# Merged counts and comparisons on VectorE, and a GpSimd wait for landed transfers, in a two-layer graph network kernel

## What is computed

```python
# layer 0: a max over the edges of each src
msg = relu(x@W_m1.T[src] + x@W_m2.T[dst] + edge_attr@W_me.T + biases)
msg = relu(msg @ W_net.T + b_net)
agg = segment_max(msg, src)            # 0 where a node has no edge
x   = layernorm(x + x@W_o1.T + b_o1 + agg@W_o2.T + b_o2)
# layer 1: a sum over the edges of each dst
h   = gelu(concat(x[src], x[dst]) @ eW1 + eb1) @ eW2 + eb2
agg = segment_sum(h, dst)
x   = layernorm(x + gelu(concat(x, agg) @ nW1 + nb1) @ nW2 + nb2)
```

## Time and profile before

| | |
|---|---|
| median of 3 runs | 3422.4 us (3416.85 to 3427.18) |
| the profiled execution | 3427.05 us, its span 3425.3 us |
| TensorE busy | 2516.2 us, 73%; mean granted clock 0.81 of full |
| GpSimd busy | 1717.8 us, 50% |
| VectorE busy | 1784.0 us, 52% |
| ScalarE busy | 1400.1 us, 41% |
| DMA | 294.49 MB, mean 86 GB/s |

### The profile page before, as it was taken

The page is one execution under the profiler, slowest core; times in us unless marked ns, Lnnn a source line. Parts: engine busy times, 40 slices in busy tenths (PEclk is TensorE's granted clock), DMA queues, the critical chain, the costliest instruction groups (busy, mean ns, idle before and its releaser), DMA issues. The chain is left out here.

```text
span 3425.3 us, 78136 instructions
## 1 busy us (share of the span) xinstructions
PE 2516.2 (73%) x20612; PEld 2180.0 (64%) x20613; DVE 1784.0 (52%) x7747; ACT 1400.1 (41%) x3974; POOL 1717.8 (50%) x1843
## 2 busy tenths in 40 slices
PE   6777765666677777778759974777777777777787
PEld 5666654555566666666547764766666677666777
DVE  7655544443355555555547752444445445454456
ACT  2344333333355555555547751232333233233334
POOL 5455544555545545554231225656655655555544
PEclk8777666766688888888879996787888878888788
DMA  7323323211133343434759931111111111111111
GB/s 205 85 73 74 75 64 83 65 34 43 51 105 111 111 111 112 119 113 138 205 163 277 280 98 42 44 40 41 42 42 40 43 40 41 39 39 40 41 32 39
DMA packets 368367, 294.49 MB, mean 86 GB/s; under 512 B 241708, under 2 KB 335986, under 8 KB 368002
## 3 DMA queue, kind: packets, MB, share of 16 engines
q1 hardware_dynamic: 138944, 129.88, 13.6%
q0 software_dynamic: 54176, 96.13, 10.0%
q10 hardware_dynamic: 175010, 65.62, 7.6%
HBM read 170.05 MB, written 127.82 MB: 87 GB/s over the span
## 5 line engine op out<-in xcount | busy, mean ns | idle before, releaser
L1386 POOL DMA_INDIRECT edge_in_src_order<-ring_u,ring_p x784 | 769.9, 982 | 728.2 <-issue 509.4
L2090 POOL DMA_INDIRECT a_rows<-src_table,src_c x782 | 739.5, 946 | 540.4 <-SPq L2106 316.5
L2213 ACT ACTIVATE h<-ps_h 128x512 f32<-128x512 f32 x208 | 124.2, 597 | 822.6 <-remote 597.5
L2134 DVE TENSOR_SCALAR ohd_f<-niota,dloc_c 128x128 f32<-128x128 bf16 x832 | 185.2, 299 | 391.0 <-remote 177.7
L2181 PE MATMUL ps_s<-ohd_f,h 128*128 128x128 f32 x1664 | 286.7, 318 | 124.1 <-issue 85.7
L2172 PE MATMUL ps_h<-bpart,dstT_b 128*128 x1664 | 300.6, 338 | 104.7 <-ACT dstT_b L2207 81.4
L1478 DVE TENSOR_TENSOR_SCAN top<-same,top,bank 96x512 f32<-96x512 bf16 x221 | 281.7, 1274 | 180.7 <-remote 104.9
L1634 PEld LDWEIGHTS bank<-m,dstT 128*128 128x128 f32 x1568 | 270.5, 248 | 161.4 <-issue 160.2
L1421 DVE TENSOR_TENSOR prior<-bank,earlier 128x512 f16<-128x512 f32 x196 | 134.9, 688 | 438.1 <-remote 384.7
L1634 PE MATMUL bank<-m,dstT 128*128 x1568 | 291.7, 335 | 87.2 <-issue 65.3
L2167 PE MATMUL ps_h<-a_rows,ident 128*128 x1664 | 282.9, 317 | 92.9 <-issue 91.7
(11 more groups left out here) (352 smaller groups left out, 5048.6 us busy)
## 6 DMA issues: line engine op xcount, KB each, us to landing
u_in<-edge_in_src_order SPq DMA_DIRECT2D x222, 192.0 KB
running_max<-row ACTq DMA_DIRECT2D x222, 192.0 KB
rowt<-src_row SPq DMA_DIRECT2D x222, 128.0 KB
running_max<-zero_rows ACTq DMA_DIRECT2D x37, 576.0 KB
same<-same_src_row SPq DMA_DIRECT2D x222, 96.0 KB
edge_in_src_order<-ring_u,ring_p POOLq DMA_INDIRECT x784
a_rows<-src_table,src_c POOLq DMA_INDIRECT x782
dge_attributes_by_column<-in_edge_attrT SPq DMA_DIRECT2D x8, 784.0 KB, 12.0
```

What stands on the lines that cost most here:

```text
L1386: pool.indirect_dma_start(u_d, bass.IndirectOffsetOnAxis(ring_p[:, j:j + 1], 0), ring_u[:, j, :], None).then_inc(sent[i % 4], 16)
L2090: pool.indirect_dma_start(a_rows[:, c % (4 * RING), :], None, a_d, bass.IndirectOffsetOnAxis(src_c[:, c:c + 1], 0)).then_inc(got[g % RING] ...
L2134: last = v.tensor_scalar(ohd[:, u, j, :], niota[:], dloc[:, u, j:j + 1], None, ALU.is_equal)
```

## The change

Four edits:

1. In the placing stage the four `tensor_tensor_reduce` of a group become one `tensor_tensor` multiply over all 4x64 counts (`picked_counts`, placed before `coarse`) and one `tensor_reduce` over the last axis (`across_steps`). `junk2` becomes fp32. `place_chain` goes up by 2 a group, not 4, and TensorE's `count` waits only until the multiply of the group in front has read `ps_cnt`.
2. GpSimd, in the placing stage, waits ahead of the third DMA of a group until all four DMAs of the group in front have landed.
3. The same in layer 1's gather.
4. In layer 1 the four comparisons of a group become one `tensor_tensor` (128x512) with both inputs broadcast.

```diff
-                junk2 = sb(until_d, "junk2", [P, 4, SL], BF16)
+                junk2 = sb(until_d, "junk2", [P, 4, SL])
@@ GpSimd, placing
                             for j in range(4 * (i % RG), 4 * (i % RG) + 4):
+                                if j % 4 == 2 and i:
+                                    pool.wait_ge(sent[(i - 1) % 4], 64 * ((i - 1) // 4 + 1))
+                                    pass_waits(pool, passed)
@@ VectorE, placing
+                        def picked_counts(i, u, n):
+                            dve.wait_ge(cnt_ready, i + 1)
+                            wait(dve, place_chain, 2 * i)
+                            v.tensor_tensor(junk2[:].rearrange("p (c j) a -> p c j a", j=2), ps_cnt[:, 0:4, :].rearrange("p (c j) a -> p c j a", j=2),
+                                            ohlo[:, u].rearrange("p c a j -> p c j a"), ALU.mult).then_inc(place_chain, 1)
+
                         def across_steps(i, u, n):
-                            dve.wait_ge(cnt_ready, i + 1)
-                            for j in range(4):
-
-                                v.tensor_tensor_reduce(junk2[:, j, :], ps_cnt[:, j, :], ohlo[:, u, j // 2, :, j % 2], 1.0, 0.0,
-                                                       ALU.mult, ALU.add, across[:, u, j:j + 1]).then_inc(place_chain, 1)
+                            dve.wait_ge(place_chain, 2 * i + 1)
+                            v.tensor_reduce(across[:, u], junk2[:], AX.X, ALU.add).then_inc(place_chain, 1)
@@ put
-                            dve.wait_ge(place_chain, 4 * (i + 1))
+                            dve.wait_ge(place_chain, 2 * (i + 1))
@@ order
-                        order = [("d", 4, scan), ("c", 3, advance), ("c", 3, same_step), ("c", 3, coarse), ("c", 4, across_steps), ("c", 3, fine),
+                        order = [("d", 4, scan), ("c", 3, advance), ("c", 3, same_step), ("c", 4, picked_counts), ("c", 3, coarse), ("c", 4, across_steps), ("c", 3, fine),
@@ TensorE, count
-                            wait(pe, place_chain, 4 * i)
+                            wait(pe, place_chain, 2 * i - 1)
@@ GpSimd, layer 1
                             for c in range(4 * g, min(4 * g + 4, NC)):
+                                if c % 4 == 2 and g:
+                                    pool.wait_ge(got[(g - 1) % RING], 64 * ((g - 1) // RING + 1))
+                                    pass_waits(pool, passed)
@@ VectorE, layer 1, onehot
-                            for j in range(4):
-                                last = v.tensor_scalar(ohd[:, u, j, :], niota[:], dloc[:, u, j:j + 1], None, ALU.is_equal)
-                            last.then_inc(oh_ready, 1)
+                            v.tensor_tensor(ohd[:, u], bcast(niota[:].unsqueeze(1), P, 4, P), bcast(dloc[:, u, :].unsqueeze(2), P, 4, P),
+                                            ALU.is_equal).then_inc(oh_ready, 1)
```

More of the change, by code:

```diff
@@ L1659, in net @@
                             if isinstance(i, int) and i == KS + 1:
-                                pe.wait_ge(place_chain, 4 * CG)
+                                pe.wait_ge(place_chain, 2 * CG)
                             pe.wait_ge(msg_ready, i + 1)
```

## The result

| | before | after |
|---|---|---|
| median of 13 runs each | 3422.4 us | 3404.6 us |
| ratio, 95% interval | | 0.9944 [0.9929, 0.996] |
| the profiled execution, its span | 3425.3 us | 3395.3 us |
| placing, first to last indirect DMA | 1484.1 us | 1465.3 us |
| layer 1, first to last indirect DMA | 1265.8 us | 1257.7 us |

The change made the kernel 18 us faster, 0.56%. The forecast was 3427 us, 5 us slower. The time lies inside the wide range (3275 to 3470 us), but outside the forecast's own (3412 to 3445 us), and the change went the other way. Of the 30 us between the two profiled executions, 19 lie in the placing stage and 8 in layer 1. The 98 gathers between these stages take the same time in both (303 and 304 us).

A forecast was written before the change was run, and what follows sets the result against it. It took long runs of GpSimd's indirect DMAs, which stall TensorE and its signals, to bound the kernel. Terms 0, +5 and 0 took the profiled 3427 us to 3432, less 4.65 gives 3427 us; range 3275 to 3470, its own 3412 to 3445.

The forecast's parts named there:

- What bounds the kernel: Both stages: long runs of GpSimd indirect DMAs hold back TensorE and its signals; layer 1 cycles at 12.5 us per two groups.
- rival A: Both stages: GpSimd's new waits break up the stall of TensorE's signals; faster, 3300 us, chance 0.29.
- The GpSimd waits at 0: Both stages: landing takes 3.28 us, within the 3.75 us before the third DMA, so waits cost 0; upper bound 180 us.
- The picked counts at +5 us: Placing stage: merged counts make `put` 0.16 us later but release TensorE's `count` 0.3 us sooner; +5 us, bounds -12 to +22.
- The comparison at 0: Layer 1: merging saves VectorE 42 us, hidden by GpSimd's run and the stall; 0, up to -42 us if uncovered.
- Rival C: Layer 1: the two-input comparison contends for SBUF ports and lengthens GpSimd's DMAs, 28 us slower, 3450 us; chance 0.07.
- Rival D: Both stages: saved VectorE time pays, 12 us from placing and half of 42 in layer 1; faster, 3389 us, chance 0.09.
- Rival B: Layer 1: landing plus restart exceeds 3.75 us, so the wait pauses GpSimd; 54 us slower, 3476 us, chance 0.12.

The follow-up runs named there:

- the looser form: Kernel before plus only GpSimd's landed waits, each for the group two in front instead of one: 3472.1 us against 3463.0, ratio 1.0018.
- c0: Kernel before with only three table-read wait values bounded below by 1: 2529.1 us, ratio 0.9999.
- the slowed kernel: Kernel before with the placing stage's eight transposes per group done five times over, slowing TensorE: 3609.7 us against 3463.0.
- chip 10: Here the kernel before took 3417.7 us; GpSimd's waits alone took 3425.1 us (1.0004), the whole change 3407.9 us (0.9966).
- chip 12: Here both merges (counts and comparison) without GpSimd's waits took 3399.1 us against the kernel before at 3427.9, ratio 0.9921.
- chip 6: Here both merges (counts and comparison) without GpSimd's waits took 3472.0 us against the kernel before at 3472.7, ratio 1.0006.

## Why the prediction was right or wrong

**What bounds the kernel.** Right for the chip that the trace came from, and the price of rival A was right as arithmetic: "with no stall layer 1 would go at GpSimd's 5.0 us a group" is what the free chips do. Wrong was to take the stall as something that every chip gives this program. That the time lies in the wide range is luck: the range was drawn down to 3275 us for rival A, which did not happen.

**The GpSimd waits at 0.** Right on held chips: 1.0004, 1.0018 with the looser form, and 9.5 us in 10 waits in the recorded trace. But it rested on one landing, "at a quiet moment". Its 3.28 us is no bad value for the middle: by the last recorded rise of each group's semaphore in the trace of c0, the landing takes 3.3 us in the median there. But a quarter of the groups take over 4.1 us, more than the 3.75 at hand, and one value can't show that. With the restart it is 5.21 us in the group shown. On held chips there is more room, since GpSimd itself pauses: it is idle 705 us ahead of this stage's DMAs in the recorded trace of after, against 252 for the kernel before on a free chip.

**Rival A** did not happen. The long runs in layer 1 are still there (82 of 7 or 8 in a row by GpSimd's lines in the timeline, 82 before), and so is "remote".

**The picked counts at +5 us.** This is the step that failed. Its durations were right, its sum was not: it had a loss of 5 us, where the stage got shorter. The edit alone was tried twice: 5.3 us faster on a free chip (0.9981 [0.9972, 0.999]), and 8.9 us faster on the slowed kernel, which doesn't clear the error. The upper bound took it that a later `put` delays the cycle; the lower one took TensorE's 40 waits for `across` as all that an earlier release of `count` can give, 12 us. Neither describes the stage: placing got 19 us shorter in the recorded pair and is 22 us shorter on chip 10 with waits and merges than with the waits alone.

By the starts of GpSimd's DMAs in the timeline, the runs are no shorter with the merge: broken at 1.6 us from start to start, there are 49 of more than four in the stage before, 52 with the waits alone and 50 after. What shrinks is the time between the groups. From the last DMA of a group to the first of the next it takes 5 us or more 57 times before (347 us in all) and 50 times with the waits alone (311 us), but 42, 38 and 47 times (271, 245 and 293 us) with the merged counts (recorded after, chip 10, chip 12). On chip 6, where the merges gained nothing, it is 53 times (332 us). TensorE's late starts marked "issue" go the same way: 298 us before and 281 with the waits alone; 263, 254 and 259 with the merges, 297 on chip 6. These sums go with the length of the stage; they don't say what shortened it.

The step to mend is the bound on the gain: it took the waits that the trace happens to show, 40, where the release of `count` is passed by all 195 groups (0.3 us each by the prediction's own estimate, up to 59 us), and TensorE is seen to be there early enough to wait twice as long for VectorE. But on chip 6, without a gain, it waits so too (71 us for the multiply, 47 for `across` with the waits alone on chip 10), so an earlier TensorE is not enough. That it is this release that gained, and not the 0.15 us that VectorE saves a group, is argued and not shown; the two were not tried apart. (The 0.15 us: the four operations in the earlier trace rows and their accumulator reads below make 191 us for 195 groups, the two new groups 162.)

```profile
L1428 DVE DVE_READ_ACCUMULATOR2_ANT across<- 128x1 f32 x780 | 64.6, 83 | 0.0
```

So the step that failed is known; what shortened the stage on held chips stays open, as does why chip 6 shows no gain.

**The comparison at 0.** Right on a free chip (1.0008). On held ones it can't be told: layer 1 is 4 us shorter on chip 10 and 8 in the recorded pair, and the same program varied by 8 us.

**Rival C** had the sign of the DMA's length right and its size wrong, 5 ns for 36.

**Rival D** had the direction (3389; measured 3405), but two thirds of it were to come from layer 1, 21 of 33 us. Most came from the placing stage, where D allowed 12 us and 19 to 22 were measured.

**Rival B** had the mechanism right: it "decides from 3.75 us on". Its place and its price were wrong (54 us in layer 1; measured 0 there and 101 in placing), and its condition, as it turned out, is the chip.

Of all versions the two merges without the waits are the one to keep: 0.9987 to 0.9994 on free chips, 0.9921 and 1.0006 on held ones, while the whole change costs 4% on free ones.

## What to carry to other kernels

Put a wait for landed transfers behind an engine's queue only with a margin read from the busiest stretch of the trace, not from its end, and look at the spread of the landings and not at one of them. Ask too what gives the engine its slack: here it was a stall that other chips don't have, and without it the "free" wait cost 104 us. Where an edit releases another engine sooner, count the groups that pass the release, not the waits that the trace happens to show. Measure a small change on more than one chip: both merges were 0.8% faster on one and equal on another, and with the waits they were 0.3 to 0.6% faster or 4% slower.

## What the runs showed of the hardware

- One kernel, seven numbered chips, two times: 2528 to 2532 us on three, 3418 to 3473 us on four. The granted clock was 0.94 on the first and 0.80 to 0.81 on the second. What makes a chip be of one kind or the other no run shows.
- On the held kind TensorE does 4 instructions in 20 us while GpSimd issues gathers one behind the other; on the free kind it does 195, with the same gathers at the same 1.25 us.
- On a free chip the scatter of the placing stage lands late enough to hold back a third DMA 3.8 us on in 96 of 195 groups (100 us); the gather of layer 1 never does.
- GpSimd's scatter instruction takes 975 to 982 ns on free chips in the six traces with the merged counts and 982 to 985 in the four without. Its gather of layer 1 takes 951 to 953 ns on held chips with the merged comparison and 945 to 947 without.
